# Half packs at the ends of the small-head attentions, and the causal query blocks in the order 1, 3, 2, 0

## What is computed

```python
scores = einsum('bhqd,bhkd->bhqk', q, k) * 8 ** -0.5      # causal in layer 1: scores[k > q] = -1e30
attn   = softmax(scores, axis=-1)
out    = einsum('bhqk,bhkd->bhqd', attn, v)               # 16 heads of size 8
```

## Time and profile before

| | before |
|---|---|
| median of 3 runs | 2239.74 us |
| the profiled execution's own time | 2239.87 us |
| its span in the profile | 2238.1 us |
| mean granted clock of TensorE | 0.898 of full speed |
| busy: PE, DVE, ACT, POOL | 1884.7, 1600.8, 1364.8, 301.3 us |
| a0a: first maximum, last OD copy, end of its last multiply | 83.87, 746.62, 758.08 us |
| a1a: the same | 1678.91, 2097.37, 2108.83 us |

### The profile page before, as it was taken

How to read it: one execution, slowest core, us unless ns; L and a number is a source line. 1 busy time by engine, 2 the same in 40 slices (tenths; PEclk the granted TensorE clock), 3 DMA queues, 4 the chain that set the end, 5 groups by cost and what they waited for, 6 DMA issues and landing times. The chain is left out here.

```text
span 2238.1 us, 40233 instructions
## 1 busy us (share of the span) xinstructions
PE 1884.7 (84%) x16064; PEld 928.5 (41%) x16064; DVE 1600.8 (72%) x2303; ACT 1364.8 (61%) x2538; POOL 301.3 (13%) x463
## 2 busy tenths in 40 slices
PE   7679999999999579568888999999476999999675
PEld 2112222222222268534566777777211232334375
DVE  4799999999994443435765677776559988886334
ACT  3259989989899433234544566665342887877321
POOL 2000000000000151413321211111200000000023
PEclk7579999999999779879999999999666999999777
DMA  5000000000000169500000000000100000000074
GB/s 156 1 1 7 4 6 5 7 4 4 6 4 6 41 203 305 162 2 0 1 1 1 1 1 1 1 1 1 49 1 1 5 7 4 7 9 9 11 256 164
DMA packets 51355, 81.34 MB, mean 36 GB/s; under 512 B 7520, under 2 KB 36192, under 8 KB 51040
## 3 DMA queue, kind: packets, MB, share of 16 engines
q1 hardware_dynamic: 46000, 70.30, 9.9%
q0 software_dynamic: 3072, 6.30, 0.9%
q10 hardware_dynamic: 2096, 2.17, 0.3%
HBM read 62.49 MB, written 11.67 MB: 33 GB/s over the span
## 5 line engine op out<-in xcount | busy, mean ns | idle before, releaser
L596 ACT ACTIVATE a0a_probs<-psum 128x512 f32<-128x512 f32 x1024 | 553.8, 596 | 108.1 <-PE psum L536 101.1
L620 DVE TENSOR_REDUCE a0a_mx<-psum 128x2 f32<-128x1024 f32 x512 | 583.2, 1207 | 9.2 <-PE psum L516 9.0
L516 PE MATMUL psum<-a_KS,a_QS 48*128 48x512 bf16 (+3 forms) x1664 | 332.8, 393 | 78.4 <-DVE a0a_mx L620 42.7
L596 ACT ACTIVATE a1a_probs<-psum 128x512 f32<-128x512 f32 (+3 forms) x640 | 304.5, 533 | 117.5 <-PE psum L536 77.9
L620 DVE TENSOR_REDUCE a1a_mx<-psum 128x2 f32<-128x1024 f32 (+2 forms) x320 | 323.6, 1059 | 52.0 <-PE psum L516 29.2
L536 PE MATMUL psum<-a_QS,a_KS 51*128 51x512 bf16 (+3 forms) x1664 | 336.2, 380 | 11.0 <-ACT a1a_probs L596 4.0
L559 PE MATMUL psum<-a0a_probs,a_V 128*16 128x256 f32 x4096 | 326.5, 390 | 8.0 <-ACT a0a_OD L585 5.5
L1584 PE MATMUL psum<-b_VW,b_ST 128*128 128x129 f32 x2176 | 257.0, 280 | 16.2 <-DVE X L1695 16.2
L1584 PEld LDWEIGHTS psum<-b_VW,b_ST 128*128 128x128 f32 x2176 | 253.9, 197 | 17.4 <-DVE X L1695 17.4
L1564 PE MATMUL psum<-b_GT,AT 128*128 128x512 f32 (+3 forms) x640 | 245.2, 537 | 16.9 <-ACT b_ST L1623 16.9
L536 PEld LDWEIGHTS psum<-a_QS,a_KS 51*128 51x128 bf16 x1664 | 87.2, 93 | 368.3 <-ACT a0a_probs L596 196.2
(11 more groups left out here) (221 smaller groups left out, 1731.2 us busy)
## 6 DMA issues: line engine op xcount, KB each, us to landing
e_W<-in_l_experts SPq DMA_DIRECT2D x46, 576.0 KB, 5.3
e_W<-in_l_experts SPq DMA_DIRECT2D x22, 768.0 KB, 5.0
yg<-e_yout SPq DMA_DIRECT2D x14, 256.0 KB, 5.9
xg<-zeros SPq DMA_DIRECT2D x2, 1472.0 KB, 9.4
a_cs<-in_rope ACTq DMA_DIRECT2D x4, 512.0 KB, 9.0
a_cs<-in_rope SPq DMA_DIRECT2D x1, 2048.0 KB, 7.9
e_xin<-xg SPq DMA_DIRECT2D x2, 896.0 KB, 8.2
AT<-in_xT SPq DMA_DIRECT2D x4, 256.0 KB, 6.0
```

The source lines that it names most:

```text
L516: mm = pe.matmul(ps[:, 2 * slot + half, 0:width], QS[rows, 2 * p + i, q_cols(qb, qt * P, P)], KS[rows, 2 * p + i, c * BLK:c * BLK + width] ...
L596: act.activation(probs[:, e % P_SLOTS, c:BLK], ps[:, S_BANK + e % S_SLOTS, c:BLK], ACT.Exp, scale=scale).then_inc(exp_done, 1)
L620: dve.tensor_reduce(mx[:, pk % 2, qt, 2 * i:2 * i + 2, c], banks, AX.X, ALU.max).then_inc(max_done, 1)
```

## The change

A pack can now be split in two *half packs*, one for each unit: two heads, the same number of steps (a *half step* has one score pair, two exponentials and the products of two heads), half the items, a turn of its own, an OD copy of its own (64 partitions), and its own transfers. In a0a the first pack (block 0, p 0) and the last (block 3, p 3) are split: 18 packs, 288 steps and 530 items instead of 16, 256 and 528. In a1a the first pack (block 1, p 0) is split, and the blocks come in the order 1, 3, 2, 0: 17 packs, 168 steps and 337 items instead of 16, 160 and 336. The rules of `Plan` are the same, with the estimate of a step by its number of heads. The diff, cut to what matters:

```diff
-    def __init__(self, causal, order):
+    def __init__(self, causal, order, split):
         self.causal, self.order = causal, order
-        self.packs = [(qb, p) for qb in order for p in range(NPACK)]
-        self.steps = [(P_, kt) for P_, (qb, p) in enumerate(self.packs) for kt in range(self.key_tiles(qb))]
+        self.packs, self.block_first = [], []
+        for qb in order:
+            self.block_first.append(len(self.packs))
+            for p in range(NPACK):
+                self.packs += [(qb, p, (0,)), (qb, p, (1,))] if (qb, p) in split else [(qb, p, (0, 1))]
+        self.block_first.append(len(self.packs))
...
-            begin.append(begin[-1] + HPP * (0.11 + 0.00085 * (BLK - self.first_col(s))))
+            begin.append(begin[-1] + len(self.heads(self.steps[s][0])) * (0.11 + 0.00085 * (BLK - self.first_col(s))))
...
+    def heads(self, pk):
+        return [2 * i + half for i in self.packs[pk][2] for half in range(2)]
...
-        for i in range(2):
+        for i in units:
...
 def shift(pk):
-                    for j in range(HPP):
+                    for n, j in enumerate(plan.heads(pk)):
...
 def gather(pk):
-                    for j in range(HPP):
+                    for j in plan.heads(pk):
...
 def product(s, half):
-                        pe.wait_ge(exp_done, HPP * (s + 1))
+                        pe.wait_ge(exp_done, plan.exp0[s + 1])
...
-                    for j in range(HPP):
-                        e = HPP * s + j
+                    for n, j in enumerate(plan.heads(pk)):
+                        e = plan.exp0[s] + n
                         mm = pe.matmul(ps[32 * j:32 * j + 2 * HD, AV_BANK, a:b], V[:, kt, HPP * p + j, :],
...
-                    row = plan.rows[s]
+                    row, units = plan.rows[s], plan.packs[plan.steps[s][0]][2]
                     for half in range(2):
-                        score(s, half)
+                        if half < len(units):
+                            score(s, units[half])
                         for item in row[half * (len(row) + 1) // 2:len(row) if half else (len(row) + 1) // 2]:
                             max_item(item)
...
 def od_copy(pk):
-                    act.activation(OD[:, p, :], ps[:, AV_BANK, :], ACT.Copy).then_inc(od_done, 1)
+                    rows = slice(32 * heads[0], 32 * heads[-1] + 32)
+                    act.activation(OD[rows, p, :], ps[rows, AV_BANK, :], ACT.Copy).then_inc(od_done, 1)
...
-                        if s == plan.first[NPACK * (k + 1)] + FINISH:
+                        if s == plan.first[plan.block_first[k + 1]] + FINISH:
                             finish(k)
...
-                small_head_attention(core, "a0a", KS, QS, V, AT, False, forward)
+                small_head_attention(core, "a0a", KS, QS, V, AT, False, forward, ((0, 0), (NB - 1, NPACK - 1)))
...
-                small_head_attention(core, "a1a", KS, QS, V, AT, True, forward[::-1])
+                small_head_attention(core, "a1a", KS, QS, V, AT, True, [1, 3, 2, 0], ((1, 0),))
```

More of the change, by code:

```diff
@@ L308 @@
 class Plan:
-    def __init__(self, causal, order):
+    def __init__(self, causal, order, split):
         self.causal, self.order = causal, order
-        self.packs = [(qb, p) for qb in order for p in range(NPACK)]
-        self.steps = [(P_, kt) for P_, (qb, p) in enumerate(self.packs) for kt in range(self.key_tiles(qb))]
+        self.packs, self.block_first = [], []
[4 more added lines that the diff above has]
+        self.block_first.append(len(self.packs))
+        self.block = [k for k in range(NB) for _ in range(self.block_first[k], self.block_first[k + 1])]
+        self.steps = [(P_, kt) for P_, pack in enumerate(self.packs) for kt in range(self.key_tiles(pack[0]))]
+        self.exp0 = [0]
+        for pk, kt in self.steps:
+            self.exp0.append(self.exp0[-1] + len(self.heads(pk)))
         self.first = {}
@@ L348, in __init__, with head_cols, uses, last_on @@
             count += item[0] == "scores"
+    def heads(self, pk):
+        return [2 * i + half for i in self.packs[pk][2] for half in range(2)]
+    def head_cols(self, pk):
+        heads = self.heads(pk)
+        return slice(heads[0], heads[-1] + 1)
+    def uses(self, pk):
+        p, units = self.packs[pk][1:]
+        return sum(1 for q in range(pk + 1) if self.packs[q][1:] == (p, units))
+    def last_on(self, pk):
+        p, units = self.packs[pk][1:]
+        return [q for q in range(pk) if self.packs[q][1] == p and self.block[q] == self.block[pk] - 1
+                and set(self.packs[q][2]) & set(units)]
     def key_tiles(self, qb):
@@ L356, in scores @@
     def scores(self, pk):
-        qb, p = self.packs[pk]
+        qb, p, units = self.packs[pk]
         out = []
-        for i in range(2):
+        for i in units:
             for qt in range(TPB):
@@ L385, in on_diagonal, with small_head_attention @@
         return self.causal and kt >= TPB * self.packs[pk][0]
-def small_head_attention(core, tag, KS, QS, V, OT, causal, order):
+def small_head_attention(core, tag, KS, QS, V, OT, causal, order, split):
     nc, ps = core.nc, core.psum
     scale = float(HD) ** -0.5
-    plan = Plan(causal, order)
+    plan = Plan(causal, order, split)
     NS, NPK = len(plan.steps), len(plan.packs)
     H2 = BLK // 2
-    TR = HPP * TERMS
+    kinds = sorted({pack[1:] for pack in plan.packs})
+    kind = lambda pk: kinds.index(plan.packs[pk][1:])
     def q_cols(qb, a, n):
@@ L461, in _ @@
                     (shift, gather)[what](pk)
-                for p in range(NPACK):
-                    sp.wait_ge(shift_in[p], 16 * HPP * NB)
-                    sp.wait_ge(gathered[p], 16 * 2 * HPP * NB)
+                for pk in range(plan.block_first[NB - 2], NPK):
+                    wait_shift(sp, pk)
+                    wait_gathered(sp, pk)
             @block.gpsimd
@@ L589, in _ @@
                     c = plan.first_col(s)
-                    for j in range(HPP):
-                        e = HPP * s + j
+                    for n in range(len(plan.heads(pk))):
+                        e = plan.exp0[s] + n
                         act.wait_ge(s_ready, e + 1)
-                        if j == 0 and s >= 2:
+                        if n == 0 and s >= 2:
                             act.wait_ge(av_done, s - 1)
@@ L613, in max_item @@
                             wait_shift(dve, pk - 2)
-                        dve.tensor_copy(mrow[:, pk % 2, :], ps[0:TR, 2 * slot, :]).then_inc(row_ready, 1)
+                        rows = slice(0, TERMS * len(plan.heads(pk)))
+                        dve.tensor_copy(mrow[rows, pk % 2, :], ps[rows, 2 * slot, :]).then_inc(row_ready, 1)
                         return
                     _, pk, i, qt, c, width = item
-                    qb, p = plan.packs[pk]
+                    qb, p, units = plan.packs[pk]
                     nch = plan.chunks(qb)
```

58 lines of the change are left out of this document (30 added, 28 removed).

## The result

The changed kernel took 2255.07 us (median of 6 runs, 2252.57 to 2259.18) against 2239.95 us for the kernel before (6 runs beside it): ratio 1.0069, 95% interval 1.0054 to 1.0084, so slower by 15.1 us. The forecast was 2261 us, slower, with a range of 2242 to 2277; sign and range were right, the loss was put 6 us too high. The profiled execution has a span of 2254.2 us, 16.1 more than before.

The account below looks back on a forecast made before the run. In a0a's middle PE and DVE were taken as full with ACT close behind; a0a +14.3 and a1a +9.2 us on 2239.87 gave 2263, lowered to a forecast of 2261 us, range 2242 to 2277.

Parts of the forecast that it names:

- The bound and the price of a half step: In a0a's middle PE and DVE full, ACT close behind; a half step without items needs 1.30 us of PE.
- The rival of a product that goes by heads: In half steps: a half step costs only ACT's 1.06 us, 2248 us in all; chance 0.13.
- The argument against it from 0.35 us for eight: On PE's product: eight instructions on 128 columns took 0.35 us, against 0.50 by the rule of 62 ns a matmul.
- a0a, head: First pack of a0a split: first score at 106.9 instead of 126.27 us, yet a lag of 6.3 us after pack (0, 1).
- The terms for the low clock and for the half steps of one item: In a0a's first two half packs: 2.0 us for PE at 0.50 clock, 1.2 us for half steps with one item.
- a0a, tail: Last packs of a0a: lag grows to 16.8 us, the last gather gives 2.5 us back; a0a +14.3 us.
- a1a, head: Start of a1a: fewer items ahead, first score at about 1699.4 instead of 1712.14 us, -12.7 us.
- block 1: In a1a: its half packs cost 35 us and its later packs carry block 3's items, 107.1 us in all, +32.3 us.
- the 2 us that I took off for them: On the whole sum: 2263 us lowered to 2261, as block 1 and the low clock were likelier too high.
- The fill-and-drain rival: At both ends of a0a and a1a's start: DVE kept full, only the last half pack's exponentials follow, 2208 us; chance 0.08.
- its own signs: For fill and drain: packs (1, 2) and (1, 3) under 20 us each, the 32 half steps at the end under 35.
- The rival of a PE that stays slow after the last turn: In a0a's last 26 half steps: PE stays at 0.50 clock, 29 us more, 2290 us; chance 0.05.

Follow-up runs that it names:

- e5_fourcol: The changed kernel with each half pack's product sent to four column groups, two heads times two halves of the queries; 2243.87 us, ratio 1.0005 to 1.0027 to the kernel before.
- e1_head: The kernel before with only the first pack of a0a split; 2245.47 us, ratio 0.9999 to 1.0030.
- e2_tail: The kernel before with only the last pack of a0a split; 2244.99 us, ratio 1.0003 to 1.0033.
- e11_early: e2_tail with the turns of the last pack's two halves due 20 us ahead instead of 10; 2244.42 us, ratio 1.0009 to 1.0037 to the kernel before.
- e10_all_halves: e5_fourcol with every a0a pack in halves and a1a as in the kernel before; 2234.59 us, ratio 0.9971 to the kernel before.

## Why the prediction was right, and where it was off

**The bound and the price of a half step** held: 1.30 us was forecast and 1.30 measured, and e5_fourcol shows that it is made of columns. That it agrees to the hundredth is luck, since its two parts were off against each other: the product was put at 1.08 us and took 0.97, the score pair at 0.22 and took 0.32 up to the next product. The forecast's own 0.21 us for 128 columns would have given the product, had the rest of 0.14 been counted once and not for each half: 4 x 0.21 + 0.14 = 0.98, and 2 x 0.21 + 0.14 = 0.56 for four column groups, where 0.55 was measured. The rival of a product that goes by heads (2248 us) falls. The rule of the Trainium skill that the prediction set beside it ("TensorE: Matmul & The Clock Gate", section "Wait — 56ns, not 53.3ns?"), 62 ns for each matmul, did not bind here: eight would be 0.50 us, and they took 0.97. The argument against it from 0.35 us for eight is weaker than I put it, because the program writes four matmuls there and the trace has two records for each: 44 ns a record, but 88 a matmul. No run shows how these matmuls are decoded.

**a0a, head.** The first score moved by 19.5 us, counted from the first maximum, as forecast (19.4), and the lag at the start of pack (0, 1) was 6.2 instead of 7.8 us. After (0, 1) it was 4.5 instead of 6.3, in e1_head 3.9 at the end. The terms for the low clock and for the half steps of one item were too high: 3.2 us together, where DVE was idle for only 1.4 of the 74.3 us from its first item behind the first score to the copy of the second half pack:

```profile
105.82:180.10 74.28, 67.42 (x458) 16.59 (x455) 72.91 (x67) 36.95 (x69) 1.70 (x8) 0.95 0.01 2
```

**a0a, tail.** The packs took 36.92, 34.75 and 49.12 us for the 36.7, 34.0 and 49.3 of the forecast; the last gather gave back 2.7 instead of 2.5. The nearness of 49.12 is partly luck too, as the same pack took 47.6 us in e2_tail with a shorter stretch at low clock. That the split of the last pack saves nothing, because ACT and PE set the pace at the end in both kernels, is borne out by e2_tail and e11_early, and most by e5_fourcol: there half steps go at ACT's pace, and (3, 1) to (3, 3) still take 111.5 us against 109.5 in the kernel before.

**a1a, head: the step that failed.** "The first score comes at about 1699.4 instead of 1712.14 us" was worked out from 1678.91, which was no first maximum. The items ahead after were sized well, 20.9 us (15.5 + 2.6 + 2.8, so 1699.8 and not 1699.4) for a measured 21.7; it is the stretch before that was taken as 33.2 us and was 41.6. From the true first maxima the items ahead took 1712.14 - 1670.52 = 41.6 us before and 1705.65 - 1684.00 = 21.7 after: -20.0 instead of -12.7. These 7.3 us are the error of the a1a sum, +9.2 for a measured +2.3. The other terms were nearer: +31.7 for block 1 (forecast +32.3; its half packs 34.2 us for 35, then 17.7, 32.1 and 22.4 for 18.6, 31 and 22.5), -11.0 for block 3's first pack without the 5.0 us of `finish` (forecast -10.4), and +1.8 in block 2, which I had put at nothing: 2.2 more in (2, 3), 0.5 less in (2, 2). With -20.0 in the place of -12.7 the sum would have been 2239.9 + 14.3 + 1.9 = 2256.1 us, which is what the profiled execution took. The terms that I had called more likely too high, block 1 and the low clock, did come out 0.6 and some 1.6 us lower, but the 2 us that I took off for them do not cover the error, which lay where I had no doubt.

**The fill-and-drain rival** (2208 us) was killed by e1_head and e2_tail as they stand, and by its own signs, 32.13 and 22.39 us for (1, 2) and (1, 3) and 49.12 for the half steps at the end. But its thought is not wrong: in e10_all_halves, where *every* pack is half as large and a half step no longer costs PE extra, both ends do shrink and the attention is 6.3 us shorter. Its condition was missing in the change: one small pack beside large ones has to carry the next large pack's items, and nearly a full step's PE time for half the heads. The first of the two is shown by e5_fourcol against e10_all_halves, whose a0a differ in nothing but which packs are split: 681.2 and 669.1 us. All packs in halves with the product in two column groups was not run. The rival of a PE that stays slow after the last turn did not come: the half steps were 2.37 us apart only just after it, and 1.30 from 729.36 us on.

Open: what sets how long the clock stays low, and its exact share in the differences of 1 to 3 us between executions of the same code.

## What to carry to other kernels

When two engines work as stages of a pipeline and are nearly equally full, making the first or the last piece smaller saves little, because the piece beside it keeps its size; count the work that the neighbours must carry in the small piece's time. Check that a smaller piece is really cheaper on the engine that fills its array side by side: leaving half of the column groups empty gave little time back here (0.97 us instead of 2 x 0.56 for all four heads), and moving another part of the same product into them did (0.55). And take the start of a stage from its first instruction, not from the first row of a stretch that cuts a group.

## What was not expected of the hardware

PE's product of two heads with 512 columns took 0.97 us in two column groups and 0.55 us when the same columns were spread over four, with eight instructions in both. A turn that follows the last maximum without other items costs twice: PE idles 2.3 us and then runs its next half steps at 1.2 GHz, 2.37 us each instead of 1.30, for a stretch that was not the same in two executions (mean clock of the seven us behind it 0.56 and 0.79). An inversion of 128 columns takes 0.94 us where 512 take 3.35, so that four pieces cost 0.9 us more than one with their multiplications.
